# A tail of single steps: the third block's ranks and location moved ahead of the fourth block's turned output rows

## The reference

```python
# first layer: a recurrence over 2048 tokens, 16 heads of width 8
state = state * (1.0 - bb * kk) + bb * (vt[..., :, None] * kt[..., None, :])
out_t = jnp.einsum('bhij,bhj->bhi', state, qt)
...
out = (out - mu) / jnp.sqrt(var + LN_EPS) * ln_g + ln_b
out = out * jax.nn.silu(x @ Wg)
return out @ Wout
# mixture: two of 8 experts for each token, 640 places for each expert
logits = xt @ w_g
top_v, top_i = jax.lax.top_k(logits, TOP_K)
...
exp_rank = jnp.cumsum(exp_mask.reshape(TOP_K * T, N_EXP), axis=0) - 1
exp_mask = exp_mask * (exp_rank < cap).astype(jnp.int32)
```

## Time and profile before

| | us |
|---|---|
| median of 3 runs | 527.0 (525.55 to 528.1) |
| profiled execution, first to last instruction (span) | 525.2 |
| TensorE busy | 441.2 (84%) |
| VectorE busy | 299.8 (57%) |
| POOL busy | 254.6 (48%) |
| ScalarE busy | 236.1 (45%) |

### The profile page before, as it was taken

How to read it: one execution, slowest core, us unless ns; L and a number is a source line. 1 busy time by engine, 2 the same in 40 slices (tenths; PEclk the granted TensorE clock), 3 DMA queues, 4 the chain that set the end, 5 groups by cost and what they waited for, 6 DMA issues and landing times.

```text
span 525.2 us, 7957 instructions
## 1 busy us (share of the span) xinstructions
PE 441.2 (84%) x2782; PEld 311.6 (59%) x2782; DVE 299.8 (57%) x713; ACT 236.1 (45%) x362; POOL 254.6 (48%) x321
## 2 busy tenths in 40 slices
PE   7688587678679799999899999888867789999980
PEld 5344254345469688888785433334346687888870
DVE  5697989997322022323677999899784302121254
ACT  4578754433121143332137999877743303423320
POOL 5357785899652874455622000020715551545461
PEclk9799977757788999999999999999987999999995
DMA  5407491992159412123523434340101121121166
GB/s 131 141 1 259 154 320 55 305 309 67 42 155 335 140 43 77 56 60 115 208 81 92 105 96 102 92 160 1 32 15 37 42 76 46 59 80 54 55 237 202
DMA packets 50327, 60.87 MB, mean 116 GB/s; under 512 B 7152, under 2 KB 29296, under 8 KB 50288
## 3 DMA queue, kind: packets, MB, share of 16 engines
q1 hardware_dynamic: 42672, 47.50, 30.3%
q0 software_dynamic: 4608, 8.47, 4.8%
q10 hardware_dynamic: 3008, 4.40, 2.5%
HBM read 29.78 MB, written 25.31 MB: 105 GB/s over the span
## 4 chain that ended last, share of the span: by engine, by line
PE 51%; DVE 8%; issue 7%; ACT 4%; POOL 3%; another core or an unknown queue 3%; DMA 2%; POOLq 0%; ACTq 0%; DVEq 0%
PE ps L1313 40%; PE ps L1317 8%; DVE feat L1237 4%; PE ps L1463 2%; POOL slots_x L480 1%; POOL read L471 1%; ACT expo L839 1%; ACT rows_x L679 1%; DMA slots_x<-rows_x,put_at 1%; DMA last_got<-chosen_y 1%; ACT xnT L575 1%; POOL decay L462 1%; DVE stats L994 0%; DMA chosen_y<-ye,y_to 0%
## 5 line engine op out<-in xcount | busy, mean ns | idle before, releaser
L532 POOL DMA_INDIRECT chosen_y<-ye,y_to x80 | 79.4, 993 | 77.0 <-DVE ye L1183 56.3
L480 POOL DMA_INDIRECT slots_x<-rows_x,put_at x64 | 62.8, 981 | 48.9 <-DVE put_at L1043 31.6
L709 ACT ACTIVATE hT<-ps 128x640 f32<-128x640 f32 x64 | 45.0, 703 | 84.9 <-issue 61.7
L1317 PE MATMUL ps<-ident 128*128 128x128 f32 x584 | 75.7, 289 | 8.8 <-issue 4.1
L1317 PEld LDWEIGHTS ps<-ident 128*128 128x128 f32 x584 | 70.8, 151 | 11.9 <-issue 6.4
L1237 DVE SCALAR_TENSOR_TENSOR feat<-expo,ps 128x1024 f32<-128x1024 f32 x64 | 76.4, 1216 | 2.5 <-ACT expo L839 2.0
L839 ACT ACTIVATE expo<-ps,minus_one 128x1024 f32<-128x1024 f32 x64 | 70.3, 1114 | 12.6 <-PE ps L1313 8.6
L1313 PE MATMUL ps<-cproj_sb,hT 128*128 128x128 f32 x640 | 74.6, 276 | 0.3
L1313 PEld LDWEIGHTS ps<-cproj_sb,hT 128*128 128x128 f32 x640 | 73.0, 192 | 0.9 <-issue 0.6
L1313 PE MATMUL ps<-xeT,cfc_sb 128*128 128x320 f32 x256 | 71.7, 433 | 2.1 <-DVE xeT L1148 2.1
L1148 DVE COPY xeT<-ps 128x640 f32<-128x640 f32 x16 | 13.2, 824 | 94.0 <-issue 47.3
(11 more groups left out here) (235 smaller groups left out, 645.9 us busy)
## 6 DMA issues: line engine op xcount, KB each, us to landing
chosen_y<-empty_rows SPq DMA_DIRECT2D x32, 256.0 KB
decay<-k_rows SPq DMA_DIRECT2D x30, 256.0 KB, 5.4
stk<-part SPq DMA_DIRECT2D x96, 64.0 KB, 2.0
slots_x<-empty_rows SPq DMA_DIRECT2D x16, 325.0 KB, 6.5
xe<-slots_x SPq DMA_DIRECT2D x16, 325.0 KB
cfc_sb<-in_L_ffn_c_fc SPq DMA_DIRECT2D x2, 2048.0 KB, 9.4
got<-chosen_y SPq DMA_DIRECT2D x8, 256.0 KB
got<-chosen_y ACTq DMA_DIRECT2D x8, 256.0 KB
```

The source lines that it names most:

```text
L480: pool.indirect_dma_start(out=slots_x[k], out_offset=bass.IndirectOffsetOnAxis(ap=put_at[:, c, kk, t:t + 1], axis=0), in_=rows_x[:, kk * N ...
L532: pool.indirect_dma_start(out=chosen_y[k], out_offset=bass.IndirectOffsetOnAxis(ap=y_to[:, b, i:i + 1], axis=0), in_=ye[:, b, i * D:(i + 1 ...
L709: act.activation(hT[:, b, f, :].rearrange("p (a n) -> p a n", a=2), ps[:, 2 + 2 * (f % 2):4 + 2 * (f % 2), 0:HALF], ACT.Gelu).then_inc(h_r ...
L1317: pe.transpose(ps[:, bank, 0:P], ident[:], ident[:])
```

## The change

On VectorE `locate` of a block goes ahead of `stats_o` of the next one; on TensorE `rank` goes ahead of `turn_o`, and the unread transposes behind the last block's `turn_o` are 16 and not 28. This holds for the first three blocks; the fourth has nothing beside it.

```diff
 (VectorE)
+                b = due(n, 18)
+                if b is not None:
+                    locate(0, b, ps[:, 5 if b < NB - 1 else 4, P:2 * P].rearrange("p (r t e) -> p r t e", r=4, e=NE),
+                           ps[:, 5, 3 * P:3 * P + 4 * TB].rearrange("p (r t) -> p r t", r=4))
                 b = due(n, 10)
                 if b is not None:
                     stats_o(b)
...
                 b = due(n, 10)
                 if b is not None:
                     ln_scale(1, b, moments_o)
-                b = due(n, 18)
-                if b is not None:
-                    locate(0, b, ps[:, 5 if b < NB - 1 else 4, P:2 * P].rearrange("p (r t e) -> p r t e", r=4, e=NE),
-                           ps[:, 5, 3 * P:3 * P + 4 * TB].rearrange("p (r t) -> p r t", r=4))
 (TensorE)
+                b = due(n, 17)
+                if b is not None:
+                    rank(0, b, 5 if b < NB - 1 else 4)
                 b = due(n, 9)
                 if b is not None:
                     if b == 0:
                         pe.wait_ge(wT_ready, 4)
                     turn_o(b)
                     if b == NB - 1:
-                        keep_warm(28, 1)
-                b = due(n, 17)
-                if b is not None:
-                    rank(0, b, 5 if b < NB - 1 else 4)
+                        keep_warm(16, 1)
```

## The result

The change made the kernel slower: 533.2 us median of 4 runs (530.76 to 535.64) against 527.0 (525.55 to 528.1), a ratio of 1.0109 with a 95% interval of 1.0069 to 1.0148. Forecast were 521.4 us and a range from 517.5 to 526.5. The profiled execution of the changed kernel took 530.76 us, the fastest of its four, with a span of 529.0 (before 525.2).

The account below looks back on a forecast made before the run. Bound: the first layer's tail (130 to 180 us), a single file of waits, including 6.04 us ending with the third block's location. Sum: -5.6 us on the 525.2 span, 519.6; plus 1.8 for the median, 521.4 us; range 517.5 to 526.5.

Parts of the forecast that it names:

- Step 6: Running scan, first two blocks: moving ranks and locations adds no VectorE work; slack 2.7 us against 1.0 delay, cost 0.
- the scan's end before 130 us: Running scan: the prediction counts as wrong if this end moves.
- Step 1: TensorE, tail: rank products ahead of the fourth block's turn run 133.8 to 134.7; cost to the turn 0.1 to 0.2 us.
- Step 2: VectorE, tail: location, 1.09 us, almost wholly hidden under the turn; statistics at 135.8 instead of 135.67, cost 0.15 us.
- Step 3: TensorE, tail: 16 unread transposes for 28 end at 139.0; cut worth about 0.9 us, only because the location wait is gone.
- Step 4: Tail: fourth block's second turn no longer waits for the location; affine step at 139.9 instead of 145.47, gain 5.6 us.
- Late signal stays: Rival, tail: rank products really take until 2.7 us after their record, or delay moves on; gain 2.9, 524.1 us; chance 0.24.
- step 5: Behind the affine step: everything moves rigidly, 0 us; third block's scatters start earlier than 145.5 and cannot be late.
- the stretch to the first expert's turn: From affine step to first expert's turn: stays 34.95 us; a different length means the clock's or the transfers' doing.
- Slower: Rival: TensorE at half clock for the 30 and the 54 unread transposes, 6.9 us more; 531.0 us; chance 0.07.
- Given back once: Rival: the 54 unread transposes ahead of the first expert lose full clock, 4.5 us more; 525.9 us; chance 0.11.
- Clock stays up: Rival, tail: projection, logits and 20 unread transposes at full clock, another 2.7 us gained; 518.7 us; chance 0.12.

Follow-up runs that it names:

- e7: Changed kernel with only the third block's ranks and location ahead, the first two blocks' at their old places, 16 unread transposes: 530.3 us, 1.0055 to the kernel before.
- e8: Changed kernel with mean and variance of the output rows in PSUM, so that VectorE's shift has one SBUF operand: 531.5 us, 1.0058 to the kernel before.
- e17: Order of e7, with POOL stopping three times in its scatter trains until a TensorE signal has come: 507.7 us, 0.994 to the kernel before (510.2 us there).
- e16: Repeat run: order of e7, third block's scatters held until the last block's tokens are gated: 525.1 us, 0.9959 to the kernel before.
- e1: Changed kernel with 28 unread transposes instead of 16, the new order kept: 510.8 us, 0.9985 to the kernel before (511.0 us there).
- e3: Changed kernel with the third block's scatters held until the last block's tokens are gated: 510.9 us, 0.9993 to the kernel before (511.0 us there).
- e2: Kernel before with 16 unread transposes instead of 28, its order kept: 509.4 us, 0.9963 to the kernel before (511.0 us there).
- e12: Kernel before with 16 unread transposes instead of 28, as e2, on a chip where the kernel before takes 527.7 us: 529.4 us, 1.0021.
- e13: Changed kernel with four small waited-for memsets of POOL behind each of the second and third blocks' scatters: 531.8 us, 1.0061 to the kernel before.
- group 1: The runs e1 to e4, all on one chip, where the kernel before takes 511.0 us.
- e5: Kernel before, run again unchanged on a chip where it takes 527.2 us: 526.5 us, 0.9981.
- e11: Changed kernel with the third block's scatters held, as e3, on a chip where the kernel before takes 527.7 us: 527.5 us, 0.9998.
- e10: Changed kernel with 60 unread transposes behind the fourth block's second turn instead of 8: 538.2 us, 1.0211 to the kernel before.
- e14: Order of e7, with the second and third blocks' scatters held until the last block's tokens are gated: 529.2 us, 1.0034 to the kernel before.
- e4: Changed kernel with no unread transposes behind the fourth block's turned output rows instead of 16: 511.2 us, 1.0008 to the kernel before (511.0 us there).
- e18: Kernel before, order and 28 unread transposes kept, with three pauses of POOL in its scatter trains: 511.1 us, 1.0011 to the kernel before (510.2 us there).

## Why the prediction was wrong, point by point

**Step 6, "Cost 0", failed: 2.4 us.** I counted the location's length, asked whether a transfer had slack, and said that the change adds no work to VectorE. It adds none; it changes beside which instruction of POOL a tiny one of VectorE stands. The earlier trace rows had both engines over 90% busy in that stretch, so the question "what is POOL doing at this instant" had to be asked of each moved instruction. e7 and e8 show the cause, each in its own way. The prediction had named the sign, the scan's end before 130 us, and it moved from 127.61 to 129.70.

**Step 1** took the choice at 133.69 as fixed. It came at 135.74 with the late scan, and `turn_o`, now behind the ranks, waited for it: 136.47 for 134.51, where I gave 0.1 to 0.2. Without the scan's loss the step costs 0.0 (e17: copy until 134.11, turn at 134.16) to 0.7 us (e16: 134.01, 134.74), by whether the choice comes well before the copy's end (133.26 in e17) or with it (134.01 in e16). Before, the fourth block's turn did not depend on the third block's choice; the new order makes it.

**Step 2** was right but for some tenths: location from 136.89 to 137.98, statistics at 138.31.

**Step 3** was too small as a delay and wrong as a gain: with 28 unread transposes e1 has affine 1.6 us later than e3 with 16 (144.00 for 142.39; 0.9 forecast), but the same time over all. In the old order, where the prediction gave the cut nothing, it gains 1.5 us on one kind of chip (e2) and nothing on the other (e12).

**Step 4, gain 5.6, failed.** The recorded end of `turn_n` was forecast for 139.9 and stands at 142.27; 2.1 us of the difference are step 6 (the last scan step at 129.70 for 127.61), the rest tenths of steps 1 and 2. The affine step starts 10.2 us after it. The rival *Late signal stays* was the right suspicion with the wrong price: I took lateness for a fixed 2.69 us that belonged to those products. It is the time for which TensorE's signals, and soon its work, are held while scatters are issued back to back: the same products are on time where the scatters are spaced (e13) or the chip is another (group 1). In the kernel before, the rank's signal released the location, and the location the next scatters: the late signal itself made the pause in the train that ended it. The early location takes that pause away, so the next signal waits for the end of sixteen scatters, not eight. My sentence in step 5, that the third block's scatters "cannot be late", looked at the wrong side: they came early, and this was the damage.

**The sum.** Forecast for the affine step was 139.9, measured 152.5: 2.1 from the scan, 0.3 from steps 1 and 2, and 10.2 from the signal. Forecast for the stretch to the first expert's turn was 34.95 us, measured 185.67 - 152.49 = 33.18: the second wait of 3.64 us is gone, since the train has ended by then, and logits and 20 unread transposes run at full clock (1.06 and 2.38 for 1.87 and 4.00); against it stand the 30 (4.86 for 3.56) and the 54 (8.88 for 6.26). So the turn comes 5.25 us later than before, not 5.6 earlier, and the span ends 3.8 us later; the other three runs took 2.3 to 4.9 us more than the profiled one, which was not traced further.

**The rival *Slower*** named 531.0 us, close to the truth by its time only. Its half clock for the 30 and the 54 did come in part, at 3.9 us of the 6.9, but was made good by the stretch between. *Given back once* and *Clock stays up* both describe something that happened, and neither decided.

**What failed in the method**: the 2.69 us were the largest unexplained thing on the path, I gave them a name and a constant size, and did not ask what else ended near them. All the rows were there: POOL's last scatter ended 1.60 us before each of the two.

## What to carry to other kernels

A wait without a releaser is not a constant of the instruction ahead of it: put the other engines' timelines beside it and see what ends shortly before, at every place where it occurs, before you move anything. When a move makes an input ready earlier, look for the pause that its lateness made; work that was spaced by it may now run in one piece. And on a stretch where VectorE and POOL are both nearly full, check each moved VectorE instruction with two SBUF operands, however small, against what POOL does at its new instant.

## What the runs showed of the hardware

On some chips TensorE is held up by indirect DMAs that GpSimd issues back to back, 1.28 us apart. The tails of the 13 traces in which it occurs (both kernels and e5 to e16 without e13) give a pattern. A signal of TensorE that is due in the first 6.1 us of a train is on time or up to 2.9 us late and still comes within the train (in the changed kernel the rank's, 4.0 us into it: 0.26 us). Of those due 6.3 us into a train or later, 17 in number, each came between 3.3 us before and 2.5 us after the end of the last scatter, so its lateness is, within these bounds, what is left of the train. A signal due up to 1.8 us after the last scatter can be late as well: three were, by 0.4 to 2.1 us (e7, e8, e11). At 2.35 us apart (e13) nothing is late. While it lasts, records of TensorE go on with their usual times for 18 (e10) and 28 (e14) instructions past the late one and then thin out, to ten in 8.4 us in e10, so a recorded end of a matmul is no proof that anyone has been told of it.

Chips differ in this. With the same trains, 1.28 us apart, no signal is late in e1 to e4, e17 and e18, where the kernel before takes 510 to 511 us, and they are late in every run but e13 where it takes 527. These signals aren't all of the 16 us between the two kinds: the kernel before with pauses (e18), on the fast kind, has the first expert's turn 5.3 us earlier than the kernel before on the other (175.1 for 180.4) and ends 14.7 us earlier. What in the chips makes the difference, and by which way GpSimd's issue reaches TensorE, stays open: no run here separates GpSimd's descriptor work from the writes that it causes.
